# A routed two-pass transformer block on one core: tokens in runs of 16 a partition, W1's products moved out of the selection, the sort's last group halved

## The reference, cut to what matters

```python
def ffn(x, W1, b1, W2, b2):                       # E = 8 experts, top 2, d = 128, dff = 512
    h = jnp.mod(x[:, :2].sum(axis=1).astype(jnp.int32), E)
    sel = jnp.stack([h, jnp.mod(h + 1, E)], axis=1)
    for e in range(E):
        w = jnp.any(sel == e, axis=1).astype(x.dtype) / 2
        acc += w[:, None] * (jnp.maximum(x @ W1[e] + b1[e], 0.0) @ W2[e] + b2[e])
    return acc
x = x + 0.5 * ffn(layernorm(x), W1, b1, W2, b2)   # pass 1; x is 16 x 512 x 128
x = x + attn(layernorm(x), ...)                   # a linear recurrence over t, between the passes
x = x + 0.5 * ffn(layernorm(x), W1, b1, W2, b2)   # pass 2
```

## Time and profile before

| | |
|---|---|
| median of 3 runs | 610.79 us (609.43 to 611.56) |
| the profiled execution's own time | 610.69 us |
| its span, first to last instruction | 609.0 us |
| TensorE products / weight loads busy | 521.4 us (86%) / 440.3 us (72%) |
| VectorE busy | 431.0 us (71%) |
| ScalarE busy | 295.6 us (49%) |
| POOL busy | 321.4 us (53%) |

### The profile page before, as it was taken

How to read it: one execution, slowest core, us unless ns; L and a number is a source line. 1 busy time by engine, 2 the same in 40 slices (tenths; PEclk the granted TensorE clock), 3 DMA queues, 4 the chain that set the end, 5 groups by cost and what they waited for, 6 DMA issues and landing times.

```text
span 609.0 us, 15987 instructions
## 1 busy us (share of the span) xinstructions
PE 521.4 (86%) x5291; PEld 440.3 (72%) x5291; DVE 431.0 (71%) x1013; ACT 295.6 (49%) x494; POOL 321.4 (53%) x409
## 2 busy tenths in 40 slices
PE   0259899999999999956799836999999999999990
PEld 0126489999999999942466614579999999999980
DVE  6895777777777777746876689457777777777761
ACT  2353655555555565512888300065565555555540
POOL 2031747777777767350016610255777677777543
PEclk9998999999999999997999967799999999999996
DMA  9997111112111112109003380011111111112100
GB/s 245 325 223 104 36 37 50 45 47 50 51 48 45 50 44 52 32 30 261 17 1 71 71 140 1 15 41 43 51 47 49 45 48 46 48 50 50 36 28 17
DMA packets 45530, 40.96 MB, mean 67 GB/s; under 512 B 5813, under 2 KB 38923, under 8 KB 45458
## 3 DMA queue, kind: packets, MB, share of 16 engines
q1 hardware_dynamic: 35378, 21.65, 16.1%
q0 software_dynamic: 9088, 17.87, 11.0%
q10 hardware_dynamic: 992, 0.44, 0.4%
HBM read 23.00 MB, written 17.83 MB: 67 GB/s over the span
## 4 chain that ended last, share of the span: by engine, by line
PE 71%; DVE 13%; issue 5%; DMA 3%; ACT 3%; POOL 2%; SPq 2%; POOLq 0%; DVEq 0%; ACTq 0%
PE ps L765 19%; PE ps L747 10%; PE ps L749 10%; PE ps L748 10%; PE ps L767 10%; PE ps L727 3%; PE ps L677 3%; PE ps L783 2%; SPq L363 2%; DVE X L1111 1%; DMA X<-in_L_attn_x 1%; DVE bn L1090 1%; POOL G L479 1%; PE ps L829 1%; DMA X<-x1d 1%
## 5 line engine op out<-in xcount | busy, mean ns | idle before, releaser
L1038 DVE SCALAR_TENSOR_TENSOR hlo<-ps,hhi 128x1024 f16<-128x1024 f32 x144 | 174.1, 1210 | 102.8 <-ACT hhi L586 102.8
L586 ACT ACTIVATE hhi<-ps 128x1024 f16<-128x1024 f32 x144 | 145.5, 1011 | 170.6 <-PE ps L749 170.6
L765 PE MATMUL ps<-w2s,hhi 128*128 x1136 | 202.3, 273 | 0.0
L479 POOL DMA_INDIRECT G<-rows,places x142 | 142.0, 1000 | 100.5 <-DVE places L994 44.6
L767 PE MATMUL ps<-w2s,hlo 128*128 x1136 | 194.9, 219 | 0.0
L747 PE MATMUL ps<-xhi,w1s 128*128 128x256 f16 (+1 forms) x736 | 168.1, 248 | 3.9 <-DVE xlo L1032 2.1
L749 PE MATMUL ps<-xhi,w1s 128*128 128x256 f16 (+1 forms) x736 | 168.0, 248 | 0.0
L748 PE MATMUL ps<-xlo,w1s 128*128 128x256 f16 (+1 forms) x736 | 168.0, 248 | 0.0
L765 PEld LDWEIGHTS ps<-w2s,hhi 128*128 128x128 f16 x1136 | 111.0, 98 | 12.1
L767 PEld LDWEIGHTS ps<-w2s,hlo 128*128 128x128 f16 x1136 | 111.1, 98 | 1.3
L487 POOL DMA_INDIRECT x1d<-O,places x71 | 71.2, 1003 | 41.6 <-issue 29.1
(11 more groups left out here) (235 smaller groups left out, 510.1 us busy)
## 6 DMA issues: line engine op xcount, KB each, us to landing
rows<-X SPq DMA_DIRECT2D x2, 2080.0 KB, 21.3
rows<-X SPq DMA_DIRECT2D x4, 1040.0 KB, 7.5
X<-in_L_attn_x SPq DMA_DIRECT2D x8, 512.0 KB, 7.2
X<-x1d SPq DMA_DIRECT2D x8, 512.0 KB, 7.2
G<-rows,places POOLq DMA_INDIRECT x142, 2.6
w1r<-in_L_ffn_W SPq DMA_DIRECT2D x1, 2048.0 KB, 10.8
x1d<-O,places POOLq DMA_INDIRECT x71, 2.3
out<-O,places POOLq DMA_INDIRECT x71, 2.3
```

The costliest lines, as they stand in the source:

```text
L479: nc.gpsimd.indirect_dma_start(out=G[tile.slot][:, s, :], out_offset=None, in_=rows, in_offset=bass.IndirectOffsetOnAxis(ap=places[:, tile ...
L586: nc.scalar.activation(hhi[tile.k][e][:, :, 0:tile.cols], H[e][:, :, 0:tile.cols], ACT.Relu).then_inc(hi_done[e], 1)
L765: nc.tensor.matmul(Y[tile.k][:, s, :], hhi[tile.k][e][:, c, tok], w, start=first, stop=False, skip_group_check=True)
L1038: v.scalar_tensor_tensor(out=hlo[tile.k][e][:, :, c], in0=H[e][:, :, c], scalar=0.0, in1=hhi[tile.k][e][:, :, c], op0=ALU.max, op1=ALU.sub ...
```

## The change

The tokens of pass 1 stand in X in runs of 16: token g*2048 + p*16 + u in partition p, column g*16 + u. `x` is read and `rows` written through views of that form (`x_g`, `rows_g`), so that a partition's part of a chunk is 8 tokens in a row in DRAM, and its part of a half of `rows` two runs of 16 whole rows. Pass 2 keeps the old order. Each pass has its own table of token numbers (`tokid[r]`).

The products of W1 leave the selection: six experts (EARLY) are done before it, behind 8 warm products; the last two come behind it, and ScalarE takes their parts after scaling W2. The square of W2 on ScalarE moves behind the six experts, and TensorE adds it up before the last group of the selection.

The last group of the selection is built and multiplied in two halves (`PIECES`), into bank 1. VectorE joins the first three groups on `perm_most` and adds the last by itself on `perm_ready`. The warm-up products in the sort of pass 2 are (30, 0, 0, 0), those behind the sorts 12 and 20.

The scaling of b2 on ScalarE moves from before the first tile to behind its high part; VectorE waits for it (`b2_ready`) at the first residual. An unused way for POOL to do the product with the token numbers (`tok_pool`) is taken out.

```diff
+    EARLY = 6
-    x_t = x.rearrange("b (t p) d -> p (b t) d", p=P)
+    x_g = x.rearrange("b t d -> (b t) d").rearrange("(g p u) d -> p g u d", p=P, u=GRP)
+        rows_g = rows[1:N + 1, :].rearrange("(g p u) d -> p g u d", p=P, u=GRP)
+        PIECES = [(g, 0, GRP) for g in range(NT // GRP - 1)] + [(NT // GRP - 1, 0, GRP // 2), (NT // GRP - 1, GRP // 2, GRP)]
...
             for c in range(NX):
-                sp.dma_start(X[:, c * XC:(c + 1) * XC, 0:D], x_t[:, c * XC:(c + 1) * XC, :]).then_inc(x_in[c], 16)
+                g, u = c * XC // GRP, c * XC % GRP
+                sp.dma_start(X[:, c * XC:(c + 1) * XC, 0:D], x_g[:, g, u:u + XC, :]).then_inc(x_in[c], 16)
...
-                sp.dma_start(rows_t[:, s, :], X[:, s, :]).then_inc(rows_out[0], 16)
+                s, gs = slice(h * NT // 2, (h + 1) * NT // 2), slice(h * NT // GRP // 2, (h + 1) * NT // GRP // 2)
+                sp.dma_start(rows_g[:, gs], X[:, s, :].rearrange("p (g u) d -> p g u d", u=GRP)).then_inc(rows_out[0], 16)
...
-            pool.wait_ge(sel_b, NT // GRP)
+            pool.wait_ge(sel_b, len(PIECES))
...
+            w_high(0)
+            for e in range(1, EARLY):
+                w_high(e)
+                w_low(e - 1)
+            w_low(EARLY - 1)
             act.wait_ge(w_in[2], 16)
             nc.scalar.activation(w2s[:, :, :, 0:P], w2r[:], ACT.Square, accum_out=sq[:, 2:3]).then_inc(sq_done, 1)
             act.wait_ge(sum_pe, 2)
             nc.scalar.activation(sums[:, 2:3], ps[:, 6, 2:3], ACT.Copy).then_inc(sum_in, 1)
-            w_high(0)
-            for e in range(1, E):
-                w_high(e)
-                w_low(e - 1)
-            w_low(E - 1)
             act.wait_ge(scale_ready, 2)
...
-            act.wait_ge(b2_sum, 1)
-            nc.scalar.activation(b2t[:], b2t[:], ACT.Copy, scale=0.25).then_inc(b2_ready, 1)
+            for e in range(EARLY, E):
+                w_high(e)
+            for e in range(EARLY, E):
+                w_low(e)
...
                 normalise(Tile(r, 0))
                 x_high(Tile(r, 0))
+                if r == 0:
+                    act.wait_ge(b2_sum, 1)
+                    nc.scalar.activation(b2t[:], b2t[:], ACT.Copy, scale=0.25).then_inc(b2_ready, 1)
                 normalise(Tile(r, 1))
...
-            sort_warm = (30, 6, 6, 0)
+            sort_warm = (30, 0, 0, 0)
...
+                    warm(8, 7)
                     w_times(0)
                     w_times(1)
-                    pe.wait_ge(sq_done, 2)
-                    nc.tensor.matmul(ps[:, 6, 2:3], ones[:], sq[:, 2:3], start=True, stop=True,
-                                     skip_group_check=True).then_inc(sum_pe, 1)
-                    w_times(2)
-                    w_less(0)
-                    w_times(3)
-                    w_less(1)
+                    for e in range(2, EARLY):
+                        w_times(e)
+                        w_less(e - 2)
+                    w_less(EARLY - 2)
+                    w_less(EARLY - 1)
+                last, starts = NT // GRP - 1, [(g, u) for g, u, _ in PIECES]
                 for t in range(NT):
                     g, u = t // GRP, t % GRP
-                    if u == 0 and r == 0 and g >= 1:
-                        for e in range(4 + 2 * (g - 1), min(6 + 2 * (g - 1), E)):
-                            w_times(e)
-                            w_less(e - 2)
+                    if r == 0 and t == NT - GRP:
+                        pe.wait_ge(sq_done, 2)
+                        nc.tensor.matmul(ps[:, 6, 2:3], ones[:], sq[:, 2:3], start=True, stop=True,
+                                         skip_group_check=True).then_inc(sum_pe, 1)
...
+                    if (g, u) in starts:
+                        pe.wait_ge(sel_b, r * len(PIECES) + starts.index((g, u)) + 1)
+                        pe.wait_ge(tok_ready, r * len(PIECES) + starts.index((g, u)) + 1)
+                    o = ps[:, 7, g * NB:(g + 1) * NB] if g < last else ps[:, 1, 0:NB]
...
                 ins.then_inc(perm_ready, 1)
+                if r == 0:
+                    for e in range(EARLY, E):
+                        w_times(e)
+                    for e in range(EARLY, E):
+                        w_less(e)
...
-            w_less(E - 2)
-            w_less(E - 1)
             pe.wait_ge(w_lo, E)
             pe.wait_ge(b1_in, 32)
-            warm(20)
+            warm(12)
             ffn(0)
...
             sort(1)
-            warm(30, 4)
+            warm(20, 4)
             ffn(1)
...
+                last = NT // GRP - 1
+                dve.wait_ge(perm_most, r + 1)
+                gp = ps[:, 7, 0:last * NB].rearrange("p (g n) -> p g n", n=NB)
+                link(v.scalar_tensor_tensor(out=gm[:, 0:last], in0=gp, scalar=0.0, in1=goff[:, 0:last].rearrange(
+                    "p (g a) -> p g a", a=1).to_broadcast([P, last, NB]), op0=ALU.is_gt, op1=ALU.mult))
+                link(v.tensor_tensor(gm[:, 0:last], gm[:, 0:last], gp, ALU.add))
+                link(v.tensor_reduce(g_f[:], gm[:, 0:last].rearrange("p g n -> p n g"), AX.X, ALU.add))
                 dve.wait_ge(perm_ready, r + 1)
...
+                gp = ps[:, 1, 0:NB]
+                v.scalar_tensor_tensor(out=gm[:, last], in0=gp, scalar=0.0, in1=goff[:, last:last + 1].to_broadcast([P, NB]),
+                                       op0=ALU.is_gt, op1=ALU.mult)
+                link(v.tensor_tensor(g_f[:], g_f[:], gp, ALU.add))
+                link(v.tensor_tensor(g_f[:], g_f[:], gm[:, last], ALU.add))
```

68 lines of the change are left out of this document (26 added, 42 removed).

## The result

The changed kernel takes 600.01 us (median of 4 runs, 599.84 to 600.33); the kernel before, run beside it, takes 610.95 (609.43 to 611.56). The ratio is 0.9832, with an interval of 0.9819 to 0.9845. The profiled execution of the changed kernel took 600.33 us, its span is 598.6 (609.0 before). 600.5 was forecast. Every number here is of fast runs; one run of the experiment x_staged, at 1851 us, is left out.

A forecast was written before the change was run, and what follows sets the result against it. TensorE, busy 86% of the span, was taken as the bound, lacking mainly at the start, change-over and 359 to 396. 1.0 + 2.2 + 1.0 + 6.0 = 10.2 us off 610.69 gave 600.5, range 597 to 605.5.

The forecast's parts named there:

- The front: Start of pass 1, loads of x and row statistics: longer DRAM pieces cut VectorE's waits, gaining 1.0 us.
- the long side decides: Loads of x: if the longer DRAM side sets the rate, VectorE's whole gap goes, 2.8 us.
- the short side decides: Loads of x: if the 512 B SBUF side sets the rate, nothing is gained.
- The store of `rows` and W1's products out of the selection: Before and in pass 1's selection: store gives and costs nothing, six experts' products are covered, selection ends at 54.0 instead of 58.97.
- The start of the first tile in pass 1: After pass 1's selection: first tile's transpose moves from 66.37 to 64.15, 2.2 us, bounds 1.3 and 3.9.
- The first tiles: First stretch of pass 1's tiles: gathers get more time before the w2s split, gaining 1.0 us, bounds 0 and 1.5.
- Pass 2: Second sort: no warm-ups between groups, overlapped join and shorter warm-up behind gain 6.0 us, lower bound 3.6.
- Rival 1: Warm-ups before both passes: with fewer wide products the clock may return only inside the pass; 605.3 us, chance 15%.
- Rival 2: Loads of x: the long side of a piece decides, 1.8 us more gained; 598.7 us, chance 13%.
- Rival 3: Start of pass 1: W2 scaling chain and POOL-VectorE lock leave it no gain, only pass 2 counts; 604.7 us, chance 13%.
- Rival 4: Gathers of pass 1: rows 64 KB apart instead of 4 KB land slower; 618 us, chance 4%.
- Rival 5: Whole kernel: the edits do not reach the chain; 610.5 us, chance 3%.

The follow-up runs named there:

- x_staged: Changed kernel with x loaded contiguous into free memory, statistics reading it there, and ScalarE copying each chunk into X; median 600.88 us.
- old_layout: Changed kernel with the old token layout of pass 1 and 520 B pieces in the store of `rows`; median 1.2 us from the changed kernel's.
- x_long_both: Changed kernel with x loads contiguous in SBUF too, 4 KB on both sides, output not the reference's; rank product at 26.13 us against 28.95.
- w1_in_selection: Changed kernel with W1's products back between the selection groups and without the eight warm products; last scatter to x1d at 271.55, 4.3 us later.
- sort_whole: Changed kernel with the last selection group whole and all four groups joined at once, in both passes; median 601.41 us.
- w2_low_by_memset: Changed kernel with W2's low part zeroed by memset instead of split off, so left out of the result; runs 598.34, 598.34, 599.95, 600.04 us.
- early_w2_sum: Changed kernel with TensorE's sum over W2's squares ahead of the second selection group instead of the last; median gains 0.2 us.
- warm_behind: Changed kernel with 20 and 30 warm products behind the sorts instead of 12 and 20; median 603.02 us.
- warm_in_sort2: Changed kernel with the warm-ups between the groups of the second sort back, (30, 6, 6, 0); median 605.09 us.

## Why the prediction was right, point by point

The sum was 10.2 us and the span lost 10.4. The total is closer than its terms: of the four, two came out at nearly nothing, one at twice its size. That the sum met the measured gain within 0.2 us is in good part luck: the terms missed by 2.6, 1.0, 0.9 and 0.4 us, and in both directions.

**The front: 1.0 forecast, 0 measured** against the kernel before (21.40 against 21.39); old_layout's 0.45 at the rank product is hardly outside of the spread. The step that failed is the choice of 1.0 between "the long side decides" and "the short side decides": x_long_both shows that in these loads the short side decides. The bounds, -0.5 to 2.8, held it. That W1 would come in behind x and shift with it didn't matter.

**The store of `rows` and W1's products out of the selection: as forecast.** The store moves at 433 GB/s instead of 209, and old_layout shows no gain from it. Six experts run from 32.8 to 41.2 on TensorE and ScalarE (forecast 34 to 41), the square of W2 from 41.13 to 44.84 beside the first selection group, and the selection ends at 53.97 (54.0). Put back (w1_in_selection), they cost 4.4 us.

**The start of the first tile in pass 1: 2.2 forecast, 4.84 measured.** The chain was the right one, sum, scale, w2s, experts 6 and 7, warm-up, and three of its sizes were off. The scale took 1.05 us from ScalarE's copy of the sum to POOL's last step (51.81 to 52.86) and not the 1.73 of the earlier trace rows. The difference is in POOL's first two steps, 0.22 and 0.19 us now. Before, they were longer, from POOL's timeline of the kernel before:

```profile
38.18 0.47 POOL L430 TENSOR_SCALAR sbit<-sums 128x1 int32<-128x1 int32 x1 [2.58 <-ACT sums L558]
38.74 0.61 POOL L431 TENSOR_SCALAR sbit<-sbit 128x1 int32<-128x1 int32 x1
```

They stood beside VectorE's 0.69 us steps on two tiles (L964, L965). The steps beside them now (L993, L995) take one operand from PSUM. That this is the cause is argued from the rows; no run tested it by itself.

Experts 6 and 7 took 2.1 us behind w2s (56.79 to 58.89), not 2.4. And the twelve warm products took 2.76, not 4.3: the clock had come back during the last products of W1 (0.63 over 53.8 to 56.8, 1.00 after). I had taken it to be low there, as it was in the earlier trace rows. So W1 was complete 0.9 us sooner than forecast, and 1.5 came from the clock. The second isn't safe: in sort_whole and w1_in_selection the same twelve took 4.29 and 4.87, in the other ten experiments and the changed kernel they ran at the higher clock (2.76, and in proportion). Nor does it count for much: sort_whole, with the 4.3 us of the forecast, began pass 1 2.3 us later than the changed kernel and ended it 0.3 later (last scatter at 267.50 against 267.21). The 4.84 lie above the upper bound of 3.9, which took the gathers to be last at 62.2; the first tile was in fact normalised at 61.39.

**The first tiles: 1.0 forecast, 0.1 measured** (third transpose 8.32 after the first before, 8.24 now). The step that failed is that the gathers would have more time ahead of the first tile. From the first gather to the first transpose were 5.13 us before (61.24 to 66.37); I had 6.95 (57.2 to 64.15), and it became 5.19 (56.34 to 61.53), because the first tile came 2.6 us sooner than forecast and the gathers only 0.9. The "four microseconds more" of the prediction were too many by its own numbers, which give 1.8 (6.95 less 5.13): the first tile was to move too. So the fourth and fifth gather met the splits of w2s just as before. For the fourth there was nothing to gain in any case, since both it and the first split follow the places at a fixed distance (the first gather to the split took 3.55 us before, 61.24 to 64.79, and 3.54 now, 56.34 to 59.88). Only the second split follows the first tile, and so it is the fifth gather that can slip in ahead of it. w2_low_by_memset and early_w2_sum are the proof: where the fifth gather takes 0.94, the third transpose is at +7.05. This term and the one before it are not independent: warm_behind, with the first transpose at 63.62, has +7.05 as well. Whatever of the first tile's start lies ahead of the gathers' pace is handed back. Of the surplus of 2.6 in the one term, 0.9 is missing in the other and 1.0 in the front, which leaves 0.7; pass 2 takes 0.4 of it back.

**Pass 2: 6.0 forecast, 5.6 measured.** The selection without warm-ups ends at 378.77, places at 379.62, 10.06 us earlier than before, of which 4.87 are pass 1's: 5.2, as forecast (5.1). The first tile was normalised in time. The warm-up took 6.99 us instead of 6.15, with twelve products at the lower clock instead of nine; warm_in_sort2 puts a price on both sides of it, 4.0 us net for the twelve taken out. The same twenty took between 5.83 and 6.99 us in the kernels with twenty there, and the changed kernel's is one of the two longest. It hardly matters: the first tile was normalised at 384.96, 29.90 behind the rank product, and no shorter warm-up could have given more than 0.5.

**Rival 1, the clock comes back only inside the pass**, did not come true. In pass 2 the clock came back later than forecast, which cost the warm-up 0.8 us and not the rival's 2.4 and more: the window 378.6 to 382.6 is at 0.50, the next at 0.84, and the pass itself begins at 1.00. In pass 1 it was 1.00 from 56.8 on. The rival's sentence on the products of 71 columns reads more into the earlier trace rows than they hold: the clock was 1.00 in the earlier trace rows while 32 such products ran, and in pass 2 of the same kernel it fell near 374, just as they began, behind 5.01 us in which TensorE had nothing to do. **Rival 2** is refuted by x_long_both. **Rival 3** had the lock right in place, 1.0 us at L1002, but not in effect: the places, 55.82, came 0.8 later than forecast and the warm-up covered it. Its other half, that pass 1 gains nothing, is wrong by 4.9. **Rival 4**, slower gathers, is refuted by the landing times, 2.5, 2.6 and 3.7 against 2.5, 2.6 and 3.6. **Rival 5** has nothing for it.

What stays open: what decides whether the clock is back before the warm-up of pass 1. The changed kernel and sort_whole have the same products of W1 there, and in the one the clock rose before 56.8, in the other after 61.5; no run here tells why.

## What to carry to other kernels

These loads ran at the rate of their shorter side (285 GB/s with 4 KB in DRAM and 512 B in SBUF, 389 with 4 KB on both), so look at the tile's own rows before giving a view of DRAM longer pieces. One case with a short side in SBUF is all that was run. Work that has an idle stretch elsewhere on the same engine should be moved out of a chain even if it looks small: the products of W1, put back into the selection, cost 4.3 us, 2.1 of them by the clock of the warm-up behind. And behind a first tile that is released early, look at once for what the next two wait for, here an index gather that stands still behind a two-operand step of VectorE (2.65 us instead of 0.95). And look at the end of a pass, not at its beginning: a first tile 2.3 us later ended the pass 0.3 us later.

## What the hardware showed that I had not expected

The products of 71 columns take the same time at both clocks: 4.49 us for 32 at 54.48 in the earlier trace rows and 4.55 in pass 2 of the changed kernel. Windows, first of the kernel before, then of the changed kernel:

```profile
54.50:59.00 4.50, 4.50 (x34) 4.40 (x33) 0.00 (x0) 1.27 (x3) 0.00 (x0) 1.00 0.09 17
```

```profile
368.00:378.60 10.60, 9.15 (x65) 8.56 (x66) 10.05 (x16) 0.00 (x0) 0.00 (x0) 0.50 0.01 2
```

The clock stayed at 0.50 through all 64 of them in pass 2, and twelve of the 512-column products behind ran before it was back at 1.00; in pass 1 of the kernel before it was 1.00 all through 32 of them. So in pass 2 the low clock cost the selection nothing, and was paid for by the twelve products behind.

The lock showed itself in four places: a two-operand step of VectorE beside POOL's addition, 1.23 against 0.23 us; POOL's addition behind VectorE's split, 2.51 against 0.46; the split behind the larger of POOL's additions, 3.22 against 2.34; an indirect gather behind the same split, 2.65 against 0.95. A memset by VectorE of the same tile (0.91 us) held up no gather.

SyncE's own time for a transfer went with its pieces: the store of `rows` kept its queue for 9.47 us before the change and 0.89 after, with a sixteenth of the pieces, and 9.21 again in old_layout. The first of the small transfers of b1 behind it held the queue for 11.35 us before and 0.78 after. In both kernels the warm-up waits for ScalarE last and not for these.
